# The DMA queue of a relative-position attention: stores first, four DRAM slots, the next head's loads one per unit

## What is computed

```python
rel_pos = jnp.arange(L)[None, :] - jnp.arange(L)[:, None] + (MAX_LEN - 1)
rel_k = relative_k[rel_pos]
rel_v = relative_v[rel_pos]
scores = jnp.einsum('bhld,bhrd->bhlr', Q, K) * scale
scores = scores + jnp.einsum('bhld,lrd->bhlr', Q, rel_k)
attn = jax.nn.softmax(scores, axis=-1)
out = jnp.einsum('bhlr,bhrd->bhld', attn, V)
out = out + jnp.einsum('bhlr,lrd->bhld', attn, rel_v)
```

## Time and profile before

| | us |
|---|---|
| median of 3 runs (3958.41 to 4023.03) | 3974.83 |
| the profiled execution | 4002.26 |
| its span | 4000.5 |
| first and last copy of T (line 1039) | 182.7 and 3382.1 |

### The profile page before, as it was taken

How to read it: one execution, slowest core, us unless ns; L and a number is a source line. 1 busy time by engine, 2 the same in 40 slices (tenths; PEclk the granted TensorE clock), 3 DMA queues, 4 the chain that set the end, 5 groups by cost and what they waited for, 6 DMA issues and landing times. The chain is left out here.

```text
span 4000.5 us, 177840 instructions
## 1 busy us (share of the span) xinstructions
PE 3468.4 (87%) x65430; PEld 2705.7 (68%) x65430; DVE 2470.0 (62%) x7245; ACT 2646.1 (66%) x5852; POOL 2748.4 (69%) x3015
## 2 busy tenths in 40 slices
PE   7488989898989898989898989899989899799991
PEld 4266767676767676666676767677767677559990
DVE  6366667666667666656675666666667666544443
ACT  3277777777767776767676777777778777224440
POOL 0187878787878787878787888787888788550006
PEclk9689999999989999989898999998999999659995
DMA  8765656565656565656565656565666565542224
GB/s 270 239 200 171 192 176 193 178 186 179 187 174 191 175 193 170 188 170 188 169 194 163 188 179 193 175 193 181 187 184 191 176 186 175 186 166 65 65 62 134
DMA packets 345830, 703.29 MB, mean 176 GB/s; under 512 B 58009, under 2 KB 157186, under 8 KB 343826
## 3 DMA queue, kind: packets, MB, share of 16 engines
q1 hardware_dynamic: 338706, 673.92, 54.5%
q0 software_dynamic: 6144, 16.79, 1.3%
HBM read 343.02 MB, written 347.46 MB: 173 GB/s over the span
## 5 line engine op out<-in xcount | busy, mean ns | idle before, releaser
L839 POOL TENSOR_TENSOR pt_near<-pt_full,pt_near 128x512 f16<-128x512 f32 (+3 forms) x2176 | 2000.8, 948 | 633.1 <-DVE pt_near L1140 565.6
L1047 ACT ACTIVATE pt_full<-pb,exp_bias 128x512 f32<-128x512 f32 x2048 | 1312.6, 693 | 582.0 <-PE pb L931 545.6
L1120 DVE TENSOR_REDUCE part_max<-pb 128x1 f32<-128x512 f32 (+3 forms) x1376 | 771.8, 575 | 513.0 <-DMA skewed<-rel_scratch 317.9
L1116 DVE CUSTOM_DVE_ANT_0 near_sum<-pb,skewed 128x512 bf16<-128x512 f32 (+3 forms) x1216 | 676.2, 572 | 339.3 <-PE pb L889 304.4
L983 PE MATMUL pb<-pt_near,table_high 128*128 128x64 f16 (+6 forms) x18432 | 873.7, 190 | 1.6 <-DVE rel_out L1163 0.8
L983 PE MATMUL pb<-pt_near,table_low 128*128 128x64 f16 (+6 forms) x9216 | 857.7, 191 | 0.0
L983 PEld LDWEIGHTS pb<-pt_near,table_high 128*128 128x128 f16 x18432 | 829.7, 99 | 1.9 <-DVE rel_out L1163 0.9
L983 PEld LDWEIGHTS pb<-pt_near,table_low 128*128 128x128 f16 x9216 | 800.3, 99 | 0.2 <-issue 0.2
L923 PE MATMUL pb<-ident,skewed 128*128 128x128 f32 x3840 | 674.8, 296 | 109.4 <-issue 54.2
L1039 ACT COPY rel<-pb 128x384 f32<-128x384 f32 x1024 | 439.4, 485 | 285.7 <-DMA rel_scratch<-rel 239.3
L957 PEld LDWEIGHTS pb<-v_head,pt_near 128*128 128x128 f16 x13440 | 435.3, 97 | 201.2 <-issue 138.7
(11 more groups left out here) (182 smaller groups left out, 4046.4 us busy)
## 6 DMA issues: line engine op xcount, KB each, us to landing
skewed<-rel_scratch SPq DMA_DIRECT2D x256, 576.0 KB, 4.8
rel_scratch<-rel SPq DMA_DIRECT2D x416, 319.5 KB, 5.3
rel_scratch<-rel SPq DMA_DIRECT2D x320, 320.0 KB, 4.6
skewed<-rel_scratch SPq DMA_DIRECT2D x64, 512.0 KB, 4.5
skewed<-rel_scratch SPq DMA_DIRECT2D x64, 448.0 KB, 3.9
k_stack<-planes_scratch SPq DMA_DIRECT2D x192, 96.0 KB, 5.1
planes_scratch<-planes SPq DMA_DIRECT2D x64, 256.0 KB, 4.2
rel_scratch<-rel SPq DMA_DIRECT2D x64, 256.0 KB, 4.5
```

The costliest lines, as they stand in the source:

```text
L839: ins = nc.gpsimd.tensor_tensor(pt_piece(c, 1, a, z, near), pt_full[e][:, (a - 4 * g) * P:(z - 4 * g) * P], pt_piece(c, 0, a, z, near), AL ...
L1047: nc.scalar.activation(pt_full[e][:, :], x_ps[e % 2][:, :], ACT.Exp, bias=exp_bias[:, 0:1]).then_inc(s_exp, 1)
L1116: ins = nc.vector.tensor_tensor_reduce(out=near_sum[:, col:col + z - a], in0=src, in1=skewed[k % 4][:, col:col + z - a], scale=1.0, scalar ...
L1120: ins = nc.vector.tensor_reduce(best, src, axis=AX.X, op=ALU.max)
```

## The change

- SyncE's step k now begins with the store of unit k (wait for T of unit k on the chip), and only then comes the load of unit k - 1 (wait for its store to land and for the turned scores of unit k - 5).
- `rel_scratch` has four slots in place of two, so the store of unit k waits for the load of unit k - 4 in place of that of unit k - 2.
- The next head's queries are loaded at c = 5 to 10, one piece each, and its keys at c = 10 to 15, one piece each (both at c = 10); before, both at c = 5 to 10. Queries and keys have semaphores of their own, and TensorE waits for the queries before the head's first product with the table and for the keys before the head's first scores, three units later.
- For the very first head the six query pieces are issued ahead of the six key pieces, in place of in turn.

The number of transfers and their bytes stay as they were. The core of the diff:

```diff
             def step(it, k):
+                u = k
+                if exists(it, u):
+                    sp.wait_ge(s_ge, it * (2 * STEP) + 2 * u + 2)
+                    sp.nop(nofuse=True)
+                    if u >= 4:
+                        sp.wait_ge(s_gr[u % 4], uses(it, u - 4, 4, 16))
+                        sp.nop(nofuse=True)
+                    for to, a, w in rel_pieces(u % NB):
+                        sp.dma_start(hbm["rel_scratch"][u % 4, :, to:to + w], rel[u % 2][:, a:a + w]).then_inc(s_gw[u % 2], 16)
                 u = k - 1
                 if exists(it, u):
...
                     w = blocks(u % NB) * P
-                    sp.dma_start(skewed[u % 4][:, 0:w], skew_src(u % 2, w)).then_inc(s_gr[u % 4], 16)
-                u = k
-                if exists(it, u):
-                    sp.wait_ge(s_ge, it * (2 * STEP) + 2 * u + 2)
-                    sp.nop(nofuse=True)
-                    if u >= 2:
-                        sp.wait_ge(s_gr[(u - 2) % 4], uses(it, u - 2, 4, 16))
-                        sp.nop(nofuse=True)
-                    for to, a, w in rel_pieces(u % NB):
-                        sp.dma_start(hbm["rel_scratch"][u % 2, :, to:to + w], rel[u % 2][:, a:a + w]).then_inc(s_gw[u % 2], 16)
-                if LOAD0 <= k % NB < LOAD0 + 6 and exists(it, (k // NB + 1) * NB):
+                    sp.dma_start(skewed[u % 4][:, 0:w], skew_src(u % 4, w)).then_inc(s_gr[u % 4], 16)
+                if LOAD0 <= k % NB and exists(it, (k // NB + 1) * NB):
+                    head, j = k // NB + 1, k % NB - LOAD0
...
-                    load_stacks(sp, it, head, [k % NB - LOAD0])
-                    if k % NB == LOAD0:
+                    if j < 6:
+                        load_queries(sp, it, head, [j])
+                    if j >= 5:
+                        load_keys(sp, it, head, [j - 5])
+                    if j == 0:
...
-                    pe.wait_ge(s_stk[(k // NB) % 2], it * STK + (k // NB // 2 + 1) * STK)
+                    pe.wait_ge(s_qin[(k // NB) % 2], it * STK + (k // NB // 2 + 1) * STK)
...
+                if c == 0 and pair == 0:
+                    pe.wait_ge(s_kin[b], it * STK + (k // NB // 2 + 1) * STK)
...
-        hbm["rel_scratch"] = nc.dram_tensor("rel_scratch", (2, P, RELW), FP32, kind="Internal").ap()
+        hbm["rel_scratch"] = nc.dram_tensor("rel_scratch", (4, P, RELW), FP32, kind="Internal").ap()
```

More of the change, by code:

```diff
@@ L602, in attend @@
         o_ps, s_ps = psum[6][:, 0:HALF_C * VW], psum[6][:, HALF_C * VW:HALF_C * (VW + DK)]
-        s_stk = [sem(f"b_stacks{i}") for i in range(2)]
+        s_qin = [sem(f"b_queries{i}") for i in range(2)]
+        s_kin = [sem(f"b_keys{i}") for i in range(2)]
         s_vi = [sem(f"b_v_in{i}") for i in range(2)]
@@ L694, in tile_rows, with load_queries @@
             return slice(tile * ROW_TILE, tile * ROW_TILE + n)
-        def load_stacks(sp, it, head, planes=range(6)):
+        def load_queries(sp, it, head, parts=range(6)):
             b = head % 2
-            for j in planes:
+            for j in parts:
                 s, tile = j % 3, j // 3
@@ L703, in load_stacks, with load_keys @@
                 sp.dma_start(q_stack[b][r0:r0 + DK, :],
-                             hbm["planes"][0, Q_PLANES[s], rows, b * L:(b + 1) * L]).then_inc(s_stk[b], 16)
+                             hbm["planes"][0, Q_PLANES[s], rows, b * L:(b + 1) * L]).then_inc(s_qin[b], 16)
+        def load_keys(sp, it, head, parts=range(6)):
+            b = head % 2
+            for j in parts:
+                s, tile = j % 3, j // 3
+                rows = bass.ds((it + head // 2) * DK, DK)
+                r0 = tile * ROW_TILE + DK * s
                 keys = hbm["planes"][1:1 + KINDS, K_PLANES[s], rows, b * L + tile * HALF_L:b * L + (tile + 1) * HALF_L]
-                sp.dma_start(k_stack[b][r0:r0 + DK, :, :], keys.rearrange("v d n -> d v n")).then_inc(s_stk[b], 16)
+                sp.dma_start(k_stack[b][r0:r0 + DK, :, :], keys.rearrange("v d n -> d v n")).then_inc(s_kin[b], 16)
         def load_v(sp, it, head):
@@ L712, in load_v @@
             sp.dma_start(v_in[b][:, :, :], src.rearrange("o p n d -> p (o n) d")).then_inc(s_vi[b], 16)
-        STK = 12 * 16
+        STK = 6 * 16
         def near_block(half, part, c, d, a, z):
@@ L747, in _ @@
             sp.nop(nofuse=True)
-            load_stacks(sp, 0, 0)
+            load_queries(sp, 0, 0)
+            load_keys(sp, 0, 0)
             load_v(sp, 0, 0)
             def step(it, k):
+                u = k
[7 more added lines that the diff above has]
+                        sp.dma_start(hbm["rel_scratch"][u % 4, :, to:to + w], rel[u % 2][:, a:a + w]).then_inc(s_gw[u % 2], 16)
                 u = k - 1
@@ L761, in step @@
                     w = blocks(u % NB) * P
-                    sp.dma_start(skewed[u % 4][:, 0:w], skew_src(u % 2, w)).then_inc(s_gr[u % 4], 16)
-                u = k
-                if exists(it, u):
-                    sp.wait_ge(s_ge, it * (2 * STEP) + 2 * u + 2)
-                    sp.nop(nofuse=True)
-                    if u >= 2:
-                        sp.wait_ge(s_gr[(u - 2) % 4], uses(it, u - 2, 4, 16))
-                        sp.nop(nofuse=True)
-                    for to, a, w in rel_pieces(u % NB):
-                        sp.dma_start(hbm["rel_scratch"][u % 2, :, to:to + w], rel[u % 2][:, a:a + w]).then_inc(s_gw[u % 2], 16)
-                if LOAD0 <= k % NB < LOAD0 + 6 and exists(it, (k // NB + 1) * NB):
-                    head = k // NB + 1
-                    if head >= 2 and k % NB == LOAD0:
+                    sp.dma_start(skewed[u % 4][:, 0:w], skew_src(u % 4, w)).then_inc(s_gr[u % 4], 16)
+                if LOAD0 <= k % NB and exists(it, (k // NB + 1) * NB):
+                    head, j = k // NB + 1, k % NB - LOAD0
+                    if head >= 2 and j == 0:
                         for s in s_x:
```

## The result

The changed kernel takes 3747.21 us (median of 4 runs, 3741.51 to 3756.96). Four runs of the kernel before, timed beside it, have a median of 3977 us; the ratio is 0.9439, with a 95% interval of 0.9397 to 0.9481: 230 us less. The profiled execution took 3739.7 us of span, 4000.5 before.

A forecast was written before the change was run, and what follows sets the result against it. SyncE's queue, walking behind its own store landings, was taken as the bound. Two heads were to fall from 202.6 to 189.5 us; 15.5 x 13.1 = 203 us off 3975 gave 3770, range 3680 to 3895.

The forecast's parts named there:

- The bound: SyncE's queue in attention: each store waits for the previous store's landing, a closed loop of 6.74 us from load to load.
- marks of 30 and 60 us: Signs of being right: ScalarE's wait for stores under 30 us, VectorE's for `skewed` under 60.
- Store first: SyncE's store goes out some 0.2 us after its copy; the 6.7 us loop goes, ScalarE's 239.3 us wait nearly vanishes.
- Load second: SyncE's load, issued after the next unit's store, may take 7.1 to 8.6 us; landing taken as 6.2, VectorE's wait nearly nothing.
- mirrored pair: Nearest timeline row for the load's landing: a store issued 0.57 us behind a load in SyncE's queue, landing in 6.2 us.
- rival with a late load: Two rivals in units 6-15: load landing in 8.5 us, 3870, chance 0.13; landing up to 10.1 us, 4070, chance 0.05.
- Four slots: The store waits for a load issued three steps earlier, costing nothing; with two slots that load lands about when it is due.
- Keys later: Next head's keys, last sent at step 15, first used at step 19, against 5.1 us to land: costed at nothing.
- The first head: At the start, queries are there some 3 us earlier, but the first scores need the keys anyway: counted as nothing.
- The sum per two heads: Attention's forecast for an even and an odd head: 189.5 us against 202.6, 13.1 less.
- the loop's entry: In the odd head's units 6-8, where TensorE stands 5.39 us for instructions; those units were left unchanged at 21.4 us.
- The rival in which nothing happens: SyncE's lateness is a shadow of engines that could go no faster: 3975 us, chance 0.09.

The follow-up runs named there:

- narrow pair: The kernel before and the changed kernel, each with transfers of T cut to a few columns, same instructions, order and waits: 3736.7 us and 3732.41 us.
- one-step-later run: The changed kernel with the load of unit k - 2 in place of k - 1 at step k: 4546.41 us, ratio 1.1374.
- narrow kernel of the old order: The kernel before with its transfers of T cut to a few columns, same instructions, order and waits: 3736.7 us, ratio 0.9348.
- values spread: The changed kernel with GpSimd's eight stages for the next head's values one per unit at units 8 to 15, not two at 7 to 10: 3702.62 us.

## Why the prediction was right, point by point

- **The bound** was named rightly. The loop store, landing, load, next store is gone from the timeline; SyncE waits for copies, stores go out 0.14 us after them (0.5 was the mark), and the two waits for T's DMAs are under the marks of 30 and 60 us. Two marks were missed on the good side: units 9-15 were to take 41 to 43.5 us and took 40.95 and 40.12, and the load was to land in near 6.2. The narrow pair shows that it was the landing in the loop and nothing else of the order. What the account of the bound left out is that the loop cost on two sides. It read the odd head's 7.1 us a unit as the queue's pace, but the loop's beat was 6.74; TensorE was busy 45.38 of 49.80 us there at a granted clock of 0.83.
- **Store first** was costed at the full gain and is the largest part, 4.2% alone.
- **Load second**: the room was worked out well (the one-step-later run), the landing was not. It was taken as 6.2 from the mirrored pair; it is 5.2 in the median of the wide ones. The step that was off is the mirror: in the old order the store was issued 0.57 us behind a load and had nearly all of it in front. In the new one the store goes out 1.5 us ahead of the load (968.58 and 970.06 above) and lands in 3.1, so only half of it is still in the way. There was more room than thought, and neither rival with a late load came near.
- **Four slots** were said to carry the first part. True and mis-stated in size: without them the new order with the new schedule still has 4.8 of the 5.6 per cent, because the load's landing, 4.6 us in the median, makes a loop of 5.6 to 6.3 us (an estimate: 4.6 and the 1.0 to 1.7 from store to load in the head above), little over what the engines take. And the prediction saw no worth in them apart from the order, where they have 1.7%.
- **Keys later** was costed at nothing. In the changed kernel that is right (3755 against 3747, not told apart). In the kernel before it is worth 2.1%, most of it in the odd heads' units 9-15, where the schedule adds transfers and the clock came back; what brings it about isn't shown.
- **The first head**: 3 us earlier and counted as nothing; the first copy came 5.5 us earlier.
- **The sum per two heads** was 189.5 against 185.4. The terms, forecast and measured: units 1-5, 56.3 and 57.2; units 6-8, 36.9 and 36.5; units 0, 12.3 and 10.6; units 9-15, 84.0 and 81.1. Two were mis-sized. Unit 0 was left at 6.16 us although its TensorE time of 5.88 was work at a granted clock of 0.72; at full clock TensorE is busy 5.14 and the unit takes 5.28, and units 1-5 give 0.46 back in the even head; that they had caught up on a late unit 0 before is a reading, not shown. The other is the odd head's units 9-15, 42.5 against 40.1: the forecast held that the lower clock level after the loop's entry reaches into them. It doesn't now. The granted share is 0.84 in units 6-8 and 1.00 in 9-15, where it was 0.83 before. It was the queue's waiting that kept the clock at 1.2 GHz for parts of them: the narrow kernel of the old order has the same loop with short landings, and 1.00 there. With 17.2 per pair in place of 13.1 the sum would have been 267, more than the 230 measured; the two pairs shown differ by more than the mean pairs do, 15.4, which gives 239. The copies' whole stretch shortened by 252 us in the profiled executions, of which the one before lay some 25 above the median.
- **The rival in which nothing happens**, the queue's beat as a shadow of engines that can go no faster, is out: the narrow kernels run at 3735. The fit of the Trainium skill, "DMA: Bandwidth & Descriptors", section on the anatomy of one DMA, gives 3.5 us for such a store, as an estimate (it is for the software path). That is near the 3.1 of a store that goes out ahead of its load, and far from the 5.3 it took behind one; the narrow stores, 1.6 us, are under its fixed part.

## What to carry to other kernels

In a queue that waits, look for a loop: an instruction that waits for the landing of a transfer issued by the same queue one step before puts that landing into every step. Issue what is ready first, put the wait for the landing behind it, and give the buffers enough slots that no other landing closes the loop again. Before moving a load later, work out its room in periods of the loop; and when one bound is gone, try again the edits that gave nothing before. When waits go, look at the granted clock and at TensorE's busy time beside them: here up to half of the gain was there, and edits whose gains came with the clock did not add up.

## What was not expected of the hardware

- A load behind a store lands almost as fast as one ahead of it: 5.2 us for 576 KB behind 640 KB, against 4.8 in front, while the store behind the load had paid 5.3 against 3.1. The queue's two transfers cost less in the order big write, 1.5 us, big read, than in the order read, 0.57 us, write. No run tells the order from the gap between the two.
- VectorE's rounding of `pt_full` (line 1140, 1156 now) costs more as the kernel gets faster, with the same instructions: 541.4 us before, 618.0 after, 645.5 with the values spread. Its largest form, 128x512, takes 532, 564 and 570 ns on average.

```profile
L1156 DVE CAST pt_near<-pt_full 128x512 f16<-128x512 f32 (+3 forms) x1280 | 618.0, 531 | 5.4 <-ACT pt_full L1063 5.4
```

  In the timeline two of them take 1.76 us beside GpSimd's long instructions (128x512), and 0.97 beside its short ones (128x256), GpSimd being busy both times (merged rows, which name only the first one's shape):

```profile
950.54 0.97 DVE L1156 CAST pt_near<-pt_full 128x512 f16<-128x512 f32 x2
...
961.38 1.76 DVE L1156 CAST pt_near<-pt_full 128x512 f16<-128x512 f32 x2
```

  Counted over the whole trace of the changed kernel, the 128x512 form takes 416 ns on average where GpSimd is idle all through it (142 of them), and 838 where GpSimd is busy for over 95% of it (136); before, 419 and 843. The Trainium skill, "SBUF — State Buffer", section on the two separate sides, has a pair of ports that VectorE, in its two-port modes, and GpSimd hold in turn for a whole instruction. The rows agree with that; which mode these casts run in no run here shows.
- Four slots in DRAM in place of two make the old order 1.7% faster, with store landings of 5.0 us in place of 5.3, though no wait that they remove shows in the trace. The cause is open.
- A stretch can run at a mean granted clock below 1 because of waits elsewhere in its loop: the same units had 0.91 with long landings and 1.00 with short ones, in the same order of instructions.
